# Attention slots: another order of the same units of maxima, output groups and output copies among the score products

## The reference

```
qkv  = einsum('bsd,ndh->bnsh', x, W_qkv)          # 16 heads of 16
attn = softmax(q k^T * 0.25 + causal mask)         # 1024 x 1024 per head
out  = einsum('bnqk,bnkh->bnqh', attn, v) -> reshape(B, -1, S)
y    = einsum('bds,nhd->bsd', out, W_out)          # both indices n, h summed
x    = layernorm(x + y)
x    = layernorm(x + FFN(x))                       # 9 paths, one picked per row
```

## Time and profile before

| | |
|---|---|
| median of three runs | 1507.09 us |
| the profiled execution | 1502.06 us |
| its span | 1500.3 us |
| TensorE busy | 1423.4 us, 95% |
| VectorE busy | 1102.5 us, 73% |
| ScalarE busy | 960.6 us, 64% |
| GpSimd busy | 431.4 us, 29% |
| granted TensorE clock over the span | 0.992 |

### The profile page before, as it was taken

The page is one execution under the profiler, slowest core; times in us unless marked ns, Lnnn a source line. Parts: engine busy times, 40 slices in busy tenths (PEclk is TensorE's granted clock), DMA queues, the critical chain, the costliest instruction groups (busy, mean ns, idle before and its releaser), DMA issues. The chain is left out here.

```text
span 1500.3 us, 25145 instructions
## 1 busy us (share of the span) xinstructions
PE 1423.4 (95%) x8234; PEld 656.3 (44%) x8282; DVE 1102.5 (73%) x2647; ACT 960.6 (64%) x2121; POOL 431.4 (29%) x561
## 2 busy tenths in 40 slices
PE   7999989999999999999999999999988999999995
PEld 4665543333333333333333333333324666566654
DVE  3225658888888888888888888888733888878775
ACT  4655447777777777777777777777775445455532
POOL 3443232122133133133133133123243262122312
PEclk9999999999999999999999999999999999999998
DMA  7899674223643843842842842842714521110001
GB/s 224 265 296 292 205 217 111 87 63 95 156 89 95 181 92 90 185 93 85 190 93 80 195 94 74 200 95 66 143 23 130 92 85 57 43 56 28 15 29 43
DMA packets 166752, 178.20 MB, mean 119 GB/s; under 512 B 26397, under 2 KB 135784, under 8 KB 166632
## 3 DMA queue, kind: packets, MB, share of 16 engines
q1 hardware_dynamic: 158184, 168.31, 44.2%
q10 hardware_dynamic: 8448, 8.39, 1.7%
HBM read 109.79 MB, written 66.06 MB: 117 GB/s over the span
## 5 line engine op out<-in xcount | busy, mean ns | idle before, releaser
L975 ACT ACTIVATE a_probs<-a_ps_s 128x512 f32<-128x512 f32 (+3 forms) x1536 | 648.0, 499 | 232.2 <-PE a_ps_s L1077 228.5
L176 DVE CUSTOM_DVE_ANT_0 h_space<-a_ps_m,a_causal 128x640 f32<-128x640 f32 (+5 forms) x624 | 530.3, 888 | 94.5 <-PE a_ps_m L150 91.1
L1077 PE MATMUL a_ps_s<-s_qs,s_ks 99*128 99x512 bf16 (+3 forms) x1536 | 405.6, 329 | 6.5 <-ACT a_probs L975 4.7
L150 PE MATMUL a_ps_m<-s_ks,s_qs 96*128 96x512 bf16 (+3 forms) x1440 | 347.1, 326 | 9.1 <-DVE a_mx L176 2.3
L925 POOL TENSOR_SCALAR_AFFINE_SELECT a_probs<-a_probs 128x512 f32<-128x512 f32 x256 | 163.0, 637 | 664.6 <-ACT a_probs L975 664.6
L1035 PE MATMUL a_ps_o<-a_probs,s_vq 128*32 128x512 f32 (+3 forms) x3072 | 327.6, 497 | 10.1 <-POOL a_probs L925 4.2
L1077 PEld LDWEIGHTS a_ps_s<-s_qs,s_ks 99*128 99x128 bf16 x1536 | 137.0, 97 | 330.7 <-ACT a_probs L975 241.6
L150 PEld LDWEIGHTS a_ps_m<-s_ks,s_qs 96*128 96x128 bf16 x1440 | 122.6, 98 | 157.8 <-issue 57.9
L1547 PE MATMUL f_ps_o<-f_w,f_hm 128*128 128x256 f32 (+1 forms) x640 | 151.5, 385 | 0.9 <-DVE f_y L1454 0.9
L1547 PEld LDWEIGHTS f_ps_o<-f_w,f_hm 128*128 128x128 f32 (+1 forms) x640 | 121.5, 192 | 27.6 <-issue 8.4
L545 PE MATMUL p_ps_qk<-p_x_t,p_wqk 128*128 128x512 f32 x256 | 120.5, 600 | 0.1
(11 more groups left out here) (137 smaller groups left out, 1310.6 us busy)
## 6 DMA issues: line engine op xcount, KB each, us to landing
qk_parts<-h_space SPq DMA_DIRECT2D x64, 384.0 KB, 4.0
s_qs<-qk_parts SPq DMA_DIRECT2D x192, 128.0 KB, 2.8
s_ks<-qk_parts SPq DMA_DIRECT2D x192, 128.0 KB, 2.8
v_rows<-h_space SPq DMA_DIRECT2D x16, 896.0 KB, 6.1
s_vq<-v_rows SPq DMA_DIRECT2D x32, 448.0 KB, 4.5
f_x_in<-in_L_attn_x_dram ACTq DMA_DIRECT2D x16, 512.0 KB, 6.7
heads_out<-a_o_sb SPq DMA_DIRECT2D x128, 64.0 KB
f_x_in<-in_L_attn_x_dram SPq DMA_DIRECT2D x8, 1024.0 KB, 8.8
```

What stands on the lines that cost most here:

```text
L150: last = pe.matmul(out, self.qs[0:TROWS, j, h, q], self.ks[0:TROWS, j, h, s:s + wide], start=k == 0, stop=mask is None)
L176: taken = dve.tensor_tensor_reduce(out=shown[:, i % 2, k * CHUNK:k * CHUNK + width], in0=row, in1=self.causal[:, SEQ - width:SEQ], scale=1 ...
L975: act.activation(probs[:, st % PB, h, 0:width], ps_s[:, n % BANKS, 0:width], ACT.Exp, scale=SCALE).then_inc(exps[h % 2], 1)
L1077: pe.matmul(ps_s[:, n % BANKS, 0:width], ks[0:MROWS, j, h, kt * P:(kt + 1) * P], qs[0:MROWS, j, h, q0:q0 + width], start=True, stop=True)\
```

## The change

`UNITS` is the same set of 22 tuples in another order. Unit 2 is still the one of query tile 0. `UNIT_AT` and `OUT_AT` have new places, and the copies of outputs are no longer tied to a step's end: `KEEP_AT` names the exp behind which each is made. Copy 1 of the slot before moves from behind exp 3 to behind exp 4, copy 0 from behind exp 19 to behind exp 21. `STEPS` and `GROUPS` are written out in another way and give the same steps and groups as before.

```diff
-UNITS = [((h,), qt) for qt in range(CT, TILES) for h in range(QUAD)]
-UNITS += [(tuple(range(h, h + 2)), qt) for qt in (3, 2) for h in range(0, QUAD, 2)]
-UNITS += [(tuple(range(QUAD)), 1)]
+UNITS = [((0, 1, 2, 3), 1), ((0,), 7), ((0, 1, 2, 3), 0), ((3,), 7), ((0, 1), 3), ((2,), 6), ((1,), 4), ((3,), 4),
...
-        UNIT_AT = [0, 2.5, 4, 6, 7, 11.5, 13.5, 16, 19, 20.5, 22, 23.5, 25, 27, 29.5, 32, 33, 35, 36.5, 39.5, 43, 44.5]
-        OUT_AT = [4, 8, 12, 15, 19, 23, 29, 32, 35, 40, 44, 47]
+        UNIT_AT = [3, 4.5, 7.5, 11, 11.5, 17, 20.5, 22, 23.5, 25, 26.5, 27, 31, 32, 34, 35, 38, 40.5, 43.5, 44.5, 47, 48.5]
+        OUT_AT = [5, 8, 14, 19, 22, 25, 29, 32, 37, 41, 45, 48]
+        KEEP_AT = (21, 4)
...
-                            if st == 0 and not (isinstance(t, int) and t == 0):
-                                keep_o(t - 1, (j - 1) % 2, 1, sent_before(*((b, j - 1) if j else (b - 1, QUADS - 1))))
-                            if st == CT:
-                                keep_o(t, j % 2, 0, sent_before(b, j))
+                                if n == KEEP_AT[1] and t:
+                                    keep_o(t - 1, (j - 1) % 2, 1,
+                                           sent_before(*((b, j - 1) if j else (b - 1, QUADS - 1))))
+                                if n == KEEP_AT[0]:
+                                    keep_o(t, j % 2, 0, sent_before(b, j))
```

More of the change, by code:

```diff
@@ L43 @@
 EPS = 1e-5
-UNITS = [((h,), qt) for qt in range(CT, TILES) for h in range(QUAD)]
-UNITS += [(tuple(range(h, h + 2)), qt) for qt in (3, 2) for h in range(0, QUAD, 2)]
-UNITS += [(tuple(range(QUAD)), 1)]
+UNITS = [((0, 1, 2, 3), 1), ((0,), 7), ((0, 1, 2, 3), 0), ((3,), 7), ((0, 1), 3), ((2,), 6), ((1,), 4), ((3,), 4),
+         ((0, 1), 2), ((0,), 4), ((1,), 7), ((3,), 6), ((3,), 5), ((2, 3), 3), ((2,), 7), ((0,), 6),
+         ((1,), 5), ((2, 3), 2), ((0,), 5), ((2,), 4), ((1,), 6), ((2,), 5)]
 TURN = 2
-UNITS.insert(TURN, (tuple(range(QUAD)), 0))
+assert UNITS[TURN][1] == 0
 NU = len(UNITS)
@@ L845, in attend_stage @@
         o_sb, o_kept, out_sent = residual.o_sb, residual.o_kept, residual.out_sent
-        STEPS = [(c, kt) for c in range(CHUNKS) for kt in range(CT * (c + 1))]
+        STEPS = [(0, 0), (0, 1), (0, 2), (0, 3), (1, 0), (1, 1), (1, 2), (1, 3), (1, 4), (1, 5), (1, 6), (1, 7)]
         NST = len(STEPS)
-        UNIT_AT = [0, 2.5, 4, 6, 7, 11.5, 13.5, 16, 19, 20.5, 22, 23.5, 25, 27, 29.5, 32, 33, 35, 36.5, 39.5, 43, 44.5]
-        OUT_AT = [4, 8, 12, 15, 19, 23, 29, 32, 35, 40, 44, 47]
+        GROUPS = [(st,) for st in range(NST)]
+        UNIT_AT = [3, 4.5, 7.5, 11, 11.5, 17, 20.5, 22, 23.5, 25, 26.5, 27, 31, 32, 34, 35, 38, 40.5, 43.5, 44.5, 47, 48.5]
+        OUT_AT = [5, 8, 14, 19, 22, 25, 29, 32, 37, 41, 45, 48]
+        KEEP_AT = (21, 4)
         PB = 3
         BANKS = 3
-        assert NU % 2 == 0 and QUAD * NST % BANKS == 0
+        assert NU % 2 == 0 and QUAD * NST % BANKS == 0 and NST % PB == 0
+        assert all(STEPS[st][0] == st // CT or st >= CT for st in range(NST)) and STEPS[CT][1] <= CT
         probs = sb("a_probs", [P, PB, QUAD, CHUNK], F32)
@@ L1031, in products @@
                         pe.wait_ge(masked, TILES * t + own)
-                    if kt == 0:
+                    first, last_one = (st in (0, CT)), (st in (CT - 1, NST - 1))
+                    if first:
                         pe.wait_ge(o_kept, CHUNKS * t + c)
@@ L1036, in products @@
                                          probs[:, st % PB, h, 0:width],
-                                         start=(kt == 0), stop=(kt == CT * (c + 1) - 1))
+                                         start=first, stop=last_one)
                     last.then_inc(pv_done, 1)
@@ L1057, in turn @@
                                 maxima.turn(pe, ps_x, (t + 1) % 2)
[L1058 to L1065, removed]
+                            for g in range(len(GROUPS)):
+                                for st in GROUPS[g - 1]:
+                                    if OUT_AT[g] == n and g:
+                                        products(t, j, st)
+                                    elif OUT_AT[g] == n and before:
+                                        products(t - 1, (j - 1) % QUADS, st)
+                                if OUT_AT[g] == n and 0 < g <= CHUNKS * KC and not after:
+                                    head.transposes(pe, ps_m[:, (g - 1) // RBANKS, (g - 1) % RBANKS, :],
+                                                    (g - 1) // KC, (g - 1) % KC, ident)
                             for i in range(NU):
@@ L1084, in _ @@
                 turn(BATCH - 1, True)
-                products(SLOTS - 1, QUADS - 1, NST - 1)
+                for st in GROUPS[-1]:
+                    products(SLOTS - 1, QUADS - 1, st)
 def feed_stage(nc, residual, head, weights, w_loaded, out):
```

## The result

| | before | changed |
|---|---|---|
| median of four runs | 1507.13 us | 1461.42 us |
| lowest to highest | 1502.43 to 1507.27 | 1460.84 to 1461.68 |
| the profiled execution, its span | 1502.06, 1500.3 | 1460.84, 1459.1 |

The changed kernel takes 0.9705 of the time before, 95% interval 0.9689 to 0.972. The forecast was 1469, the range 1459 to 1485.

What follows compares the result with a forecast made beforehand. TensorE's order was taken as the bound, with waits above a 26.9 us slot floor. 24 x 1.25 + 6 x 1.05 + 2 x 1.1 = 38.5 off 1502.06 gave 1463.6, on the median's scale 1469 us; range 1459 to 1485.

Steps and rivals of the forecast that it cites:

- Rival C: VectorE's queue of takes at the slot's opening delays TensorE at unit 6: slower, 1521 us; chance 0.04.
- j = 2: Six slots with VectorE's inversion between split and take: unit 5 waits 0.44 to 0.6; 27.55 against 28.60 us.
- Rival B: No gain: supposed waits are the issue's own rate, or both orders cost alike; 1507 us, chance 0.04.
- The ten places: Where TensorE waits in an ordinary slot of the old order, 1.33 us in all; all were to go.
- Rival A: Tight places slip, each release 0.2 later: gain only 0.65 a slot, 1485.6 us; chance 0.14.
- score 13: Score product needing exp 10, free at 6.08 when TensorE comes at 6.08: nothing to spare, the tightest place.
- The ordinary slot: Period 27.03 against 28.28 us, gain 1.25 (bounds 0.7 and 1.4), with 0.1 kept for tight places; 24 slots.
- split done at 5.33: In slots with j = 2, when VectorE's split ends; inversion and unit 3's take follow, until 7.79.
- the walk: Step-by-step timing of the new order in a slot with the old rows' prices, counted from score 0's start.
- The last slots: Two slots without units, at 25.5 us, taken as bound by exps and masks: gain 1.1 each, between 0 and 2.
- The projection stage: Stage before attention, making the units of slots 0 and 1: 0 booked, bounds -1.5 and +1.5.
- The offset: Step from the profiled execution, 1502.06 us, to the median of the runs, 1507.09: 5.03 added to 1463.6.

Runs made afterwards that it cites:

- the old units: Changed kernel with the earlier list of units in its earlier places, output groups and copies in the new ones: 1505.13 us.
- the old list: Changed kernel with only the order of the 22 unit tuples as before, in the new places, with new groups and copies: 1484.66 us.
- The thin mask: Changed kernel with GpSimd's mask of step 1 cut to 8 of 128 queries: 1456.31 us in a single execution.
- the kernel with two pairs in its first order: Changed kernel with groups 4 and 5, and 6 and 7, issued as pairs, and units, groups, copies and inversion placed anew: 1455.5 us.
- the four partial orders: Changed kernel with parts restored: copies, 1501.44 us; groups and copies, 1522.93; units and their places, 1505.13; only the order of units, 1484.66.

## Why the prediction was right, and where its terms were off

**The bound.** TensorE's order, with a floor of 26.9: right. VectorE's work cut by a third changes nothing in an ordinary slot, 0.87 more of TensorE's changes it by 0.85. Rival C, VectorE's queue, would have shown in every slot; VectorE's queue shows only where j = 2. Rival B is refuted by the copies and groups put back: the same instructions in other places take from 1461 to 1523.

**The ten places.** All gone, as walked. The copies put back bring waits of 1.27 us and a period 1.29 longer; groups and copies put back, 2.14 and 2.12; the old units, 1.39 and 1.42; the old list, 0.79 and 0.80. Waits read start to start add up to the period. Rival A needed the margins to slip; the one of 0 at score 13 lost at most 0.02, and no other place of an ordinary slot lost anything that its rows show.

**The ordinary slot: 27.03 forecast, 26.91 measured.** The 0.1 kept for the tight places wasn't spent. 24 x 0.12 = 2.9 us.

**j = 2: 27.55 forecast, 27.67 to 27.79 measured.** The place was right, the size of the wait was short. TensorE where unit 5 waits:

```profile
500.00 0.50 PE L1084 MATMUL a_ps_s<-s_qs,s_ks 99*128 99x128 bf16 x3
501.10 0.55 PE L150 MATMUL a_ps_m<-s_ks,s_qs 96*128 96x512 bf16 x2 [0.59 <-DVE a_mx L176]
```

1.10 where the ordinary slot above has 0.34 (473.09 to 473.43): 0.76, forecast 0.44 to 0.6. The step that failed is "split done at 5.33". It came 0.35 later, for two reasons. VectorE, from its take of unit 2 on (the slot's score 0 starts at 492.96):

```profile
496.75 0.69 DVE L171 TENSOR_REDUCE a_mx<-a_ps_m 128x4 f32<-128x512 f32 x1
497.35 0.27 DVE L191 TENSOR_SCALAR a_mrow<-a_ps_m 32x128 bf16<-32x128 f32 x1
497.65 0.28 DVE L193 SCALAR_TENSOR_TENSOR a_mrest<-a_ps_m,a_mrow 32x128 f32<-32x128 f32 x1
497.97 0.43 DVE L196 CAST a_mrow<-a_mrest 32x128 bf16<-32x128 f32 x1
498.43 0.28 DVE L198 TENSOR_TENSOR a_mrow<-a_mrest,a_mrow 32x128 bf16<-32x128 f32 x1
498.64 0.93 DVE L669 RECIPROCAL a_inv<-a_sums 128x128 f32<-128x128 f32 x1
```

GpSimd:

```profile
497.69 0.63 POOL L929 TENSOR_SCALAR_AFFINE_SELECT a_probs<-a_probs 128x512 f32<-128x512 f32 x1 [1.39 <-ACT a_probs L979]
```

First, the take of unit 2 starts at 3.79 of the slot, with no idle time before it, where the walk had 3.65. The walk timed it by TensorE alone; VectorE was still at unit 1's take. Rival C's own sum has that queue (1.52 + 1.18 + 1.15 = 3.85), the walk of unit 5 left it out: 0.14. Second, the third step, a CAST, takes 0.43, not 0.21: it ends at 498.40, just behind the mask's 498.32. In the old order a mask ran beside the split as well, VectorE and GpSimd before:

```profile
509.52 0.22 DVE L196 CAST a_mrow<-a_mrest 32x128 bf16<-32x128 f32 x1
```

```profile
508.89 0.63 POOL L925 TENSOR_SCALAR_AFFINE_SELECT a_probs<-a_probs 128x512 f32<-128x512 f32 x1 [1.71 <-ACT a_probs L975]
```

That mask covered the first two steps, which took no longer for it (0.27 and 0.28 in both kernels), and ended at 509.52, just as the CAST began. The new order moves the mask under the CAST. Together 0.14 + 0.21 make the 0.35. The thin mask gives 0.2 back; the 0.56 that remains lies inside the forecast's 0.44 to 0.6 only because that left room above the walk's 0.44. In the first slot with j = 2, the one of 27.79, the mask covers the last step instead and costs 0.32. In an ordinary slot the same 0.35 is there, but without the inversion unit 3's take is done at 472.98 and TensorE wants unit 5 at 473.43. 6 x 0.15 = 0.9 us the other way.

**The last slots: 1.1 each.** Measured 1.3 in the first of them (25.48 to 24.17) and 2.3 in the last (26.47 to 24.13, to the stage's last copy), so this term was short by 1.4. 24 x 1.37 + 6 x 0.9 + 1.3 + 2.3 = 41.9, the stage's 41.8. That exps and masks bound these slots was not tested; what the runs show is that the places of groups and copies set their time, the copies' places alone 1 us each.

**The projection stage: 0 booked, 0 measured.**

**The offset.** By its own trace the forecast was 1463.6 for the profiled execution, measured 1460.84: 2.8 off, which the terms above explain (2.9 + 1.4 - 0.9, less the 0.6 of the feed-forward stage). The other 5 of the miss is the step from the profiled execution of before to the median of its runs. The changed kernel's runs lie within 0.6 of its profiled one. Before's own runs ranged from 1499.8 to 1507.3 in all. Only one of them has a trace. Across the traces of all kernels the feed-forward stage, the same work in each, takes 370 to 374.7 us, at a mean granted clock from 0.98 where it is short to 0.96 where it is long (short stretches at 0.5, which is 1.2 GHz), while attention's clock is 1.00. So that before's spread comes from there is likely and not shown. Four runs of the changed kernel are few to call it steadier: those of the kernel with two pairs in its first order lie 6.4 apart.

## What to carry to other kernels

Where an engine reads as 98% busy, subtract prices from start-to-start distances before believing that it is full; the waits found that way were 5% of this slot, and in five kernels (before and the four partial orders) they added up to the period's excess within 0.04 us. An order is one object: the units alone cost 1.3%, groups and copies alone gave nothing, all but the copies 0.2%, and the whole 3%. So walk the whole new order, with every queue that shares a buffer, and start each step at the later of its input and its own engine's queue. Take a step's duration for the walk from a place where the same step has the same neighbour on the other engines, and once the waits are gone, look for what makes the instructions themselves cheaper.

## What of the hardware was not expected

Two of the four small VectorE steps of the split lengthen beside a GpSimd mask: a CAST of 32x128 from 0.21 to 0.43, and in the slot that starts at 384.44 the TENSOR_TENSOR behind it from 0.28 to 0.60, while its mask stretches from 0.63 to 0.70:

```profile
389.45 0.21 DVE L196 CAST a_mrow<-a_mrest 32x128 bf16<-32x128 f32 x1
389.70 0.60 DVE L198 TENSOR_TENSOR a_mrow<-a_mrest,a_mrow 32x128 bf16<-32x128 f32 x1
```

```profile
389.47 0.70 POOL L929 TENSOR_SCALAR_AFFINE_SELECT a_probs<-a_probs 128x512 f32<-128x512 f32 x1 [1.69 <-ACT a_probs L979]
```

A CAST that starts under the mask ends 0.07 to 0.08 behind the mask's end, in all 28 slots of the changed kernel where it does, whether it started late (0.33 long) or early (0.43); the TENSOR_TENSOR ends 0.13 behind it here. So they are held, not slowed by a factor. The two steps ahead of them, L191 and L193, read the bank a_ps_m: in before's trace they ran wholly under the mask in 30 slots and took their usual 0.27 and 0.28. The Trainium skill ("SBUF — State Buffer", Who interferes with whom) says that a VectorE copy or cast in a 2-port mode, or an operation with two SBUF inputs, shares a port pair with GpSimd, and that the later of the two is blocked until the first is done. The rows agree on the order and on the end, for the mask too, which was issued 0.02 behind the CAST and is 0.07 longer; that this CAST runs in a 2-port mode no row shows.

Two neighbouring output groups take 0.23 less than two apart (1.86 against 2.09), and so do the narrow pairs: bf16 matmuls between two groups of fp32 ones cost more than their own time. What the 0.23 consists of was not taken apart.
